# First weights of a category-conditional layer: request order of the chunks, and which of them are split

## The reference

```python
selected_W = W[cat_ids]          # (128, 512, 512) picked from (32, 512, 512)
selected_b = b[cat_ids]
y = einsum('bti,bio->bto', x, selected_W) + selected_b[:, None, :]
return x + y
```

## Time and profile before

| | us |
|---|---|
| median of 3 runs | 360.55 (360.37 to 360.61) |
| the profiled execution, whole | 360.35 |
| its span in the trace | 358.6 |
| TensorE busy | 354.1 |
| GpSimd busy | 268.4 |
| VectorE busy | 172.5 |
| ScalarE busy | 146.6 |

### The profile page before, as it was taken

The page is one execution under the profiler, slowest core; times in us unless marked ns, Lnnn a source line. Parts: engine busy times, 40 slices in busy tenths (PEclk is TensorE's granted clock), DMA queues, the critical chain, the costliest instruction groups (busy, mean ns, idle before and its releaser), DMA issues.

```text
span 358.6 us, 6784 instructions
## 1 busy us (share of the span) xinstructions
PE 354.1 (99%) x1553; PEld 289.8 (81%) x1553; DVE 172.5 (48%) x280; ACT 146.6 (41%) x262; POOL 268.4 (75%) x148
## 2 busy tenths in 40 slices
PE   8999999999999999999999999999999999999996
PEld 3888888888888888888888888888888888888884
DVE  6665445445444544544544454454445445445442
ACT  5465344334434433343443443343444343534420
POOL 3798999997747798799955999799979899934000
PEclk9999999999999999999999999999999999999999
DMA  6999998899797998889997899999998999955532
GB/s 227 361 356 387 414 368 301 310 378 355 276 321 254 351 316 290 297 309 384 329 334 249 289 380 299 326 320 375 326 316 278 364 351 323 322 201 197 180 115 90
DMA packets 43381, 109.51 MB, mean 305 GB/s; under 512 B 4817, under 2 KB 4818, under 8 KB 38610
## 3 DMA queue, kind: packets, MB, share of 16 engines
q1 hardware_dynamic: 37730, 70.01, 54.4%
q0 software_dynamic: 5328, 38.28, 30.7%
q10 hardware_dynamic: 288, 0.79, 0.6%
HBM read 75.50 MB, written 33.55 MB: 304 GB/s over the span
## 4 chain that ended last, share of the span: by engine, by line
PE 99%; DVE 0%; issue 0%
PE pA L444 96%; PE pA L398 1%; PE pA L456 1%; PE pA L469 0%; DVE os L391 0%; PE pA L415 0%; DVE fill L328 0%; PE pS L408 0%; PE pS L407 0%; PE pS L417 0%
## 5 line engine op out<-in xcount | busy, mean ns | idle before, releaser
L391 DVE TENSOR_TENSOR os<-pA,bb 128x512 f32<-128x512 f32 x128 | 88.4, 691 | 170.9 <-PE pA L444 169.8
L305 ACT ACTIVATE xh<-xs 128x512 fp32r<-128x512 f32 x127 | 80.3, 633 | 194.7 <-PE pA L444 109.1
L278 POOL TENSOR_TENSOR wl<-wr,wh 128x2048 fp32r<-128x2048 f32 x30 | 138.7, 4623 | 2.5
L444 PE MATMUL pA<-wh,xh 128*128 x508 | 135.9, 389 | 0.0
L444 PE MATMUL pA<-wl,xh 128*128 x508 | 135.8, 389 | 0.0
L444 PE MATMUL pA<-wh,xl 128*128 x508 | 135.6, 389 | 0.0
L444 PEld LDWEIGHTS pA<-wh,xl 128*128 128x128 f32 x508 | 95.4, 188 | 19.8
L444 PEld LDWEIGHTS pA<-wh,xh 128*128 128x128 f32 x508 | 95.3, 188 | 19.9 <-issue 0.2
L444 PEld LDWEIGHTS pA<-wl,xh 128*128 128x128 f32 x508 | 95.4, 188 | 19.7
L356 DVE TENSOR_TENSOR xl<-pT,xh 128x512 fp32r<-128x512 f32 x127 | 86.5, 681 | 9.4 <-ACT pT L308 9.4
L274 POOL TENSOR_SCALAR wh<-wr 128x2048 fp32r<-128x2048 f32 x30 | 57.6, 1919 | 37.1 <-PE pA L444 35.3
(11 more groups left out here) (51 smaller groups left out, 20.1 us busy)
## 6 DMA issues: line engine op xcount, KB each, us to landing
xs<-xt SPq DMA_DIRECT2D x128, 256.0 KB, 5.8
out<-os SPq DMA_DIRECT2D x128, 256.0 KB, 5.1
wr<-w POOLq DMA_DIRECT2D x29, 1024.0 KB, 7.6
bb<-bias POOLq DMA_DIRECT2D x7, 1024.0 KB, 9.3
wr<-w SPq DMA_DIRECT2D x2, 512.0 KB, 6.7
wr<-w SPq DMA_DIRECT2D x1, 1024.0 KB, 8.9
wr<-w ACTq DMA_DIRECT2D x1, 512.0 KB, 3.8
bb<-bias SPq DMA_DIRECT2D x2, 256.0 KB, 7.7
```

Source lines behind the costliest of these rows:

```text
L278: eng.tensor_tensor(wl[:, at], wr[:, c % NR, :], wh[:, at].bitcast(f32), ALU.subtract).then_inc(s_wp if c == 2 else s_w, 1)
L305: eng.activation(xh[:, i % NH, :, :], xs[:, i % NX, :, :], ACT.Copy).then_inc(s_xh, 1)
L391: eng.tensor_tensor(os[:, i % NO, :], pA[i % NA][:, :], bb[:, bass.ds(at, D)], ALU.add)._wait_ge(s_mm, i + 2).then_inc(s_fin, 1)
L444: mm = eng.matmul(pA[i % NA][:, :], xp[:, i % NH, k, :], wp[:, bass.ds(at + k * D, D)], start=(n == 0), stop=(n == 3 * KT - 1))
```

## The change

- Chunk three of the first matrix is requested by SyncE behind tile 0 and ahead of chunk four, no longer by ScalarE.
- Batch 0 makes chunks one, three and four as plain products, and only chunk two split. Its order: plain one, table load, HH and LH of two, plain three, plain four, HL of two.
- GpSimd adds the identity to chunks one and two with one operation, then to three, then to four, each at its landing; it no longer waits for s_hot.
- ScalarE makes wh in the order two, one, three, four (`HIGH`), with xh of chunk two of tile 0 behind the first; the rest of tile 0's xh, two operations, follows tile 1. VectorE follows the same order. Batch 1 runs its chunks in that order.

```diff
-    RAW = 2
-    LOW = (0, 2, 3, 1)
+    SPLIT = slice(1, 2)
+    REST = (slice(0, 1), slice(2, KT))
+    HIGH = (1, 0, 2, 3)
+    DIAG = (1, 1, 2, 3)
+    ND = 3
@@ sync
             x_load(eng, 0, ...)
+            eng.dma_start(raw(0, 2, 3), W[0, :, 2 * D:3 * D]).then_inc(s_w0[1], 16)
             eng.dma_start(raw(0, 3, KT), W[0, :, 3 * D:]).then_inc(s_w0[2], 16)
@@ gpsimd
-            eng.wait_ge(s_hot, 1)
-            for k in range(KT):
-                eye = diagonal(0, k, k + 1)
-                eng.wait_ge(s_w0[max(0, k - 1)], 16)
-                eng.tensor_tensor(eye, eye, ones_on(1), ALU.add).then_inc(s_ri, 1)
+            for n, (k0, k1) in enumerate(((0, 2), (2, 3), (3, KT))):
+                eye = diagonal(0, k0, k1)
+                eng.wait_ge(s_w0[n], 16)
+                eng.tensor_tensor(eye, eye, ones_on(k1 - k0), ALU.add).then_inc(s_ri, 1)
@@ scalar
-            eng.dma_start(raw(0, 2, 3), W[0, :, 2 * D:3 * D]).then_inc(s_w0[1], 16)
...
+            def high_w(k):
+                eng.wait_ge(s_ri, DIAG[k])
+                eng.activation(wh[:, chunk(0, k, k + 1)], raw(0, k, k + 1), ACT.Copy).then_inc(s_rh, 1)
...
-            for k in range(KT):
-                eng.wait_ge(s_ri, k + 1)
-                eng.activation(wh[:, chunk(0, k, k + 1)], raw(0, k, k + 1), ACT.Copy).then_inc(s_rh, 1)
-                if k == RAW - 1:
-                    high_0(RAW, KT, s_xh)
+            high_w(HIGH[0])
+            high_0(SPLIT, s_xh)
+            for k in HIGH[1:]:
+                high_w(k)
             high(1)
-            high_0(0, RAW, s_xb)
+            for ks in REST:
+                high_0(ks, s_xb)
@@ vector
-            for k in LOW[:1]:
-                low_w(k)
+            low_w(HIGH[0])
             eng.wait_ge(s_xh, 1)
-            low_0(RAW, KT, s_xl)
-            for k in LOW[1:]:
+            low_0(SPLIT, s_xl)
+            for k in HIGH[1:]:
                 low_w(k)
             low(1)
-            eng.wait_ge(s_xb, 1)
-            low_0(0, RAW, s_xb)
+            eng.wait_ge(s_xb, len(REST))
+            for ks in REST:
+                low_0(ks, s_xb)
@@ tensor
-                for k in range(RAW):
-                    eng.wait_ge(s_ri, k + 1)
-                    mm = eng.matmul(pA[0][:, :], xs[:, 0, k, :], raw(0, k, k + 1), start=(k == 0), stop=False)
-                mm.then_inc(s_raw, 1)
+                plain_product(0, True)
                 eng.wait_ge(s_tab, 1)
                 row(0)
-                eng.wait_ge(s_xh, 1)
-                for p, k in ((HH, 2), (LH, 2), (HH, 3), (LH, 3), (HL, 2), (HL, 3)):
...
-                mm.then_inc(s_mm, 1)
+                split_product(HH, 1)
+                split_product(LH, 1)
+                plain_product(2, False)
+                plain_product(3, False).then_inc(s_raw, 1)
+                split_product(HL, 1, stop=True).then_inc(s_mm, 1)
```

More of the change, by code:

```diff
@@ L186, in load @@
                 if i == NX:
-                    eng.wait_ge(s_xb, 2)
+                    eng.wait_ge(s_xb, 2 * len(REST))
                     eng.wait_ge(s_mm, 2)
@@ L250, in _ @@
                 eng.tensor_tensor(eye, eye, ones_on(k1 - k0), ALU.add).then_inc(s_ri, 1)
-                eng.wait_ge(s_ri, KT + 1 + h)
+                eng.wait_ge(s_ri, ND + 1 + h)
                 eng.tensor_scalar(wh[:, at], half, 1.0, 1.0, ALU.mult, ALU.mult).then_inc(s_wh, 1)
@@ L272, in _ @@
                     eng.wait_ge(s_mm, n).then_inc(s_free, 1)
-                eng.wait_ge(s_ri, KT + 1 + c)
+                eng.wait_ge(s_ri, ND + 1 + c)
                 eng.tensor_scalar(wh[:, at], wr[:, c % NR, :], 1.0, 1.0, ALU.mult, ALU.mult).then_inc(s_wh, 1)
@@ L290, in _, with high_0 @@
             eng.dma_start(raw(0, 0, 2), W[0, :, 0:2 * D]).then_inc(s_w0[0], 16)
-            eng.dma_start(raw(0, 2, 3), W[0, :, 2 * D:3 * D]).then_inc(s_w0[1], 16)
             eng.wait_ge(s_one, 3)
             eng.activation(spare[:, :], ones[:, 0:1], ACT.Copy)
-            def high_0(k0, k1, done):
+            def high_0(ks, done):
                 eng.wait_ge(s_x[0], 16)
-                eng.activation(xh[:, 0, k0:k1, :], xs[:, 0, k0:k1, :], ACT.Copy).then_inc(done, 1)
+                eng.activation(xh[:, 0, ks, :], xs[:, 0, ks, :], ACT.Copy).then_inc(done, 1)
+            def high_w(k):
+                eng.wait_ge(s_ri, DIAG[k])
+                eng.activation(wh[:, chunk(0, k, k + 1)], raw(0, k, k + 1), ACT.Copy).then_inc(s_rh, 1)
             def high(i):
@@ L357, in low, with low_0 @@
                                   ALU.subtract).then_inc(s_xl, 1)
-            def low_0(k0, k1, done):
-                eng.tensor_tensor(xl[:, 0, k0:k1, :], xs[:, 0, k0:k1, :], xh[:, 0, k0:k1, :].bitcast(f32),
+            def low_0(ks, done):
+                eng.tensor_tensor(xl[:, 0, ks, :], xs[:, 0, ks, :], xh[:, 0, ks, :].bitcast(f32),
                                   ALU.subtract).then_inc(done, 1)
             def low_w(k):
-                eng.wait_ge(s_rh, k + 1)
+                eng.wait_ge(s_rh, HIGH.index(k) + 1)
                 eng.tensor_tensor(wl[:, chunk(0, k, k + 1)], raw(0, k, k + 1), wh[:, chunk(0, k, k + 1)].bitcast(f32),
                                   ALU.subtract).then_inc(s_wd, 1)
-            for k in LOW[:1]:
-                low_w(k)
+            low_w(HIGH[0])
             eng.wait_ge(s_xh, 1)
-            low_0(RAW, KT, s_xl)
-            for k in LOW[1:]:
+            low_0(SPLIT, s_xl)
+            for k in HIGH[1:]:
                 low_w(k)
             low(1)
-            eng.wait_ge(s_xb, 1)
-            low_0(0, RAW, s_xb)
+            eng.wait_ge(s_xb, len(REST))
+            for ks in REST:
+                low_0(ks, s_xb)
             eng.wait_ge(s_tab, 1)
@@ L421, in _ @@
             HH, HL, LH = 0, 1, 2
-            first = [(p, k) for p in (HH, HL, LH) for k in LOW]
+            first = [(p, k) for p in (HH, HL, LH) for k in HIGH]
             early = [(p, k) for p in (HH, HL, LH) for k in range(KT)]
@@ L439, in batch @@
                     if i == 1 and p == HH:
-                        eng.wait_ge(s_rh, k + 1)
+                        eng.wait_ge(s_rh, HIGH.index(k) + 1)
                     if i == 1 and p == HL:
-                        eng.wait_ge(s_wd, LOW.index(k) + 1)
+                        eng.wait_ge(s_wd, HIGH.index(k) + 1)
                     xp, wp = pair[p]
@@ L453, in _, with plain_product, split_product @@
                 eng.wait_ge(s_x[0], 16)
-                for k in range(RAW):
-                    eng.wait_ge(s_ri, k + 1)
-                    mm = eng.matmul(pA[0][:, :], xs[:, 0, k, :], raw(0, k, k + 1), start=(k == 0), stop=False)
-                mm.then_inc(s_raw, 1)
+                def plain_product(k, start):
+                    eng.wait_ge(s_ri, DIAG[k])
+                    return eng.matmul(pA[0][:, :], xs[:, 0, k, :], raw(0, k, k + 1), start=start, stop=False)
+                def split_product(p, k, stop=False):
+                    if p == HH:
+                        eng.wait_ge(s_xh, 1)
+                        eng.wait_ge(s_rh, HIGH.index(k) + 1)
+                    if p == LH:
+                        eng.wait_ge(s_xl, 1)
+                    if p == HL:
+                        eng.wait_ge(s_wd, HIGH.index(k) + 1)
+                    xp, wp = pair[p]
+                    return eng.matmul(pA[0][:, :], xp[:, 0, k, :], wp[:, chunk(0, k, k + 1)], start=False, stop=stop)
+                plain_product(0, True)
                 eng.wait_ge(s_tab, 1)
                 row(0)
-                eng.wait_ge(s_xh, 1)
-                for p, k in ((HH, 2), (LH, 2), (HH, 3), (LH, 3), (HL, 2), (HL, 3)):
[L462 to L470, removed]
-                mm.then_inc(s_mm, 1)
+                split_product(HH, 1)
[3 more added lines that the diff above has]
+                split_product(HL, 1, stop=True).then_inc(s_mm, 1)
             for i in range(1, B):
```

## The result

The changed kernel takes 362.21 us (median of 10 runs, 361.57 to 363.61) against 360.87 for the kernel before beside it (10 runs, 360.37 to 361.62): ratio 1.0041, 95% interval 1.0031 to 1.005, that is 1.1 to 1.8 us more. The forecast was no change: 360.5, with eight chances in ten for 360.2 to 361.0. The profiled execution took 362.13 with a span of 360.1.

The account below looks back on a forecast made before the run. TensorE, nearly throughout, was taken as the bound, so batch 1's start sets the end. +0.18 - 0.29 + 0.05 + 0.05 = -0.01 us gave 360.5 against 360.55, eight in ten for 360.2 to 361.0.

Parts of the forecast that it names:

- Step 5: Chunk four, requested one issue later at 4.08, lands between 7.25 and 7.68; cost 0, upper end 0.05 us.
- Step 4: Chunk three, requested by SyncE behind the x tile, lands at 6.7 (bounds 6.35 and 7.25); 0.05 us charged.
- rival B: Slower: chunk three lands at 7.25 as chunk four did, plain three starts at 8.03, time 360.8; chance 0.13.
- Step 6: GpSimd's earlier add runs beside VectorE's rank chain; only the short L349 expected held, 0.05 us charged (bounds 0 and 0.67).
- Rival A: Slower: GpSimd's add holds VectorE's rank chain, hot and plain one 0.4 to 0.7 us later, 361.0; chance 0.17.
- Step 7: SyncE's later requests (x1, W1, x2, x3, bias) go out up to 0.43 us later; cost taken as 0.
- step 1: TensorE's work in batch 0 with three plain chunks and one split: 3.26 us, 0.18 more than before.
- step 2: The three-engine chain behind batch 0's last chunk goes, taking away 0.29 us of waiting; TensorE's order then ends 0.11 earlier.
- step 3: Batch 0's other inputs (xh, xl, table load) arrive in time; xl done at 7.0, wanted at 7.23; cost 0.
- E: The change does nothing for the path because the plain-product branch isn't taken; ruled out, as the trace shows L456 executed.

Follow-up runs that it names:

- c: Kernel before with only chunk three's request moved to SyncE, behind the x tile and ahead of chunk four: 362.42 us, ratio 1.0052.
- d: Changed kernel with chunks three and four as one 512 KB request behind the x tile: 362.12 us, ratio 1.0045 to the kernel before.
- e: Changed kernel with chunks three and four read from a second, chunk-contiguous copy of the first matrix: 361.67 us, ratio 1.0024 to the kernel before.
- g: Kernel before with only GpSimd's wait for the one-hot matrix (s_hot) taken away, so the adds start early: 360.96 us, ratio 1.0007.
- b: Changed kernel with chunk three requested by ScalarE again, the rest of the change kept: 361.27 us, ratio 1.0018 to the kernel before.
- f: Changed kernel with chunk three requested by ScalarE again and GpSimd waiting for s_hot again: 361.08 us, ratio 1.0017 to the kernel before.
- a: The changed kernel measured and profiled again, nothing altered: 363.36 us, ratio 1.0061 to the kernel before; a third time 362.13, 1.0042.
- s: Changed kernel, ScalarE requesting chunks one to three at start, four at 3.73; s_hot wait back, tv moved up: 361.25 us, ratio 1.0014 to kernel before.
- m: Changed kernel with chunks three and four requested as two partition halves, GpSimd waiting for both: 362.34 us, ratio 1.0048 to the kernel before.

## Why the prediction was wrong

Step 5 failed. It put chunk four's landing between 7.25 ("the bytes in front of it are the same") and 7.68, and the cost at 0. It landed at 9.14. That landing sets the start of batch 1: add, plain four and HL follow it without a gap (9.21 + 0.46, 1.13, 0.23, start at 11.13), and c shows the same landing and its price without any other part of the change. The wrong idea was to count landing by bytes and by one issue slot; d, with the same bytes in one request at 7.47, shows that bytes don't set it. What does, most likely the number of requests, no row of before had priced, and its mechanism stays open.

Step 4 was off in the same direction: 6.7 taken, 7.25 measured, the upper bound, so rival B came true. TensorE was idle for 0.29 before plain three, which the wait for chunk four covers. The 256 KB less in front brought nothing, in any kernel that asked for chunk three so (3.6 to 4.0; 3.3 in e with its contiguous rows).

Step 6: the hold is real, and on L347, which was thought safe: 0.62 in the changed kernel, up to 0.85, against 0.05 us charged. It didn't set the end, and g puts it at 0.25 us, with 0.6 as the upper end of its interval. Rival A's mechanism was there. Its time, 0.4 to 0.7 at the start of batch 0, shows in b's chain (0.53) and not in the changed kernel, where chunk four would have covered it anyway. In d, where the add starts later, at 4.83, it is below that lasts 0.69 and hot 0.29. The Trainium skill, SBUF — State Buffer, "Who interferes with whom", has GpSimd and a two-port tensor_scalar exclude each other for a whole instruction: the trace agrees, hot ending at 5.25 behind the add's 5.16, and tv lasting 2.41 behind a subtraction of 2.44. Which mode either ran in no row tells.

Step 7 took the later requests as free. x tile 1 took 4.4 instead of 3.2, but that isn't shown to come from the change: with the requests of before it took 3.2, 3.4, 4.0 and 4.6 in four profiles (before, f, b, g). In a's profile VectorE's tv, moved later with everything else, met a 2.4 us operation. That is a cost of being late which isn't in any sum of landings.

Steps 1 and 2 hold in part: 1524 matmuls take 345.5 to 345.9 whenever nothing late stops them, plain four and HL take 1.13 + 0.23, and no three-engine chain stands behind the last chunk. But the 0.11 us that they were to bring was misread from the earlier trace rows. Of the 0.29 of waiting, 1.92 - 4 x 0.43 = 0.20 lies in the plain piece, ahead of anything that chunk four releases, and only 1.44 - 6 x 0.2268 = 0.08 in the split piece, where its chain ends. So what step 2 could take away was 0.08, and with the 0.18 of step 1 the sum was 0.10 later, not 0.11 earlier. f, where chunk four is in time, starts batch 1 at 9.98, and s at 10.05; f's chain runs through step 3's xl, which the prediction had in time by 0.2 with the add at 4.55. This error is small beside step 5's and points the same way. E was rightly ruled out. The chance of slower by over 0.2% was put at 0.07; the measured interval, 0.31% to 0.5%, lies wholly in it.

## What to carry to other kernels

Price a moved request by what it stands beside, not by its bytes: at this kernel's start a second request of 256 KB behind another landed 1.7 us later than the same 512 KB did in one request (9.14 against 7.47). Where the transfer on the critical chain is already the last one, ask what the third and fourth request of the queue do before filling TensorE's time. Before crediting a change with a wait, see in which piece of the chain the wait lies. And look for short VectorE operations that a shift can push beside a long GpSimd one.

## What the runs showed of the hardware

- Of two requests of 256 KB behind an x tile the last landed at 8.4 to 9.7, one of 512 KB at 7.47; in between, in the changed kernel, the DMA engines show as busy for 1.03 and then 0.41 of half a microsecond, at 78 and 61 GB/s.
- A 2x128 tensor_scalar on VectorE took 0.22 alone, 1.07 and 2.41 beside GpSimd operations that it ended with.
- TensorE's first rise to the 2.4 GHz level is not the same in every execution: in b's profile matmuls took twice their time until past 9.4, 1.25 us in the first two pieces and 0.41 in the next, under a clock column of 1.00.
- In m TensorE's granted clock fell to 0.52 from 11 on, after 2.00 us without a matmul that ended at 9.95; weight loads then took 0.34 instead of 0.19.
